# Score and transpose banks shared by a slot's two duos, and a new order of the last attention

## The reference

```python
x = x + attention(layernorm(x), ctx, ctx)      # below
x = x + ffn(layernorm(x))

# attention: q of 32 heads, k and v of 8 heads, each k and v head serves 4 q heads
q, k, v = (query @ Wq), (ctx @ Wk), (ctx @ Wv)
q, k = rope(q, positions), rope(k, positions)          # q * cos + rotate_half(q) * sin
scores = where(mask == 0, -1e9, q @ k.T / sqrt(128))
out = (softmax(scores) @ v) @ Wo                       # (.., 32 * 128) @ (4096, 512)

# ffn
routing = softmax(x @ gate_w.T)                        # 8 experts
out = (x * (routing @ in_scale)) @ sign(weight).T * (routing @ out_scale) + bias
```

## Time and profile before

| | us |
|---|---|
| median of 3 runs | 1307.17 (1306.85 to 1307.28) |
| the profiled execution | 1309.06 |
| its span, first to last instruction | 1307.2 |
| TensorE busy | 1192.8 (91%) |
| VectorE busy | 842.7 (64%) |
| GpSimd busy | 722.0 (55%) |
| ScalarE busy | 554.0 (42%) |
| mean granted clock of TensorE | 0.978 of full |

### The profile page before, as it was taken

How to read it: one execution, slowest core, us unless ns; L and a number is a source line. 1 busy time by engine, 2 the same in 40 slices (tenths; PEclk the granted TensorE clock), 3 DMA queues, 4 the chain that set the end, 5 groups by cost and what they waited for, 6 DMA issues and landing times.

```text
span 1307.2 us, 23826 instructions
## 1 busy us (share of the span) xinstructions
PE 1192.8 (91%) x7636; PEld 957.9 (73%) x7636; DVE 842.7 (64%) x1367; ACT 554.0 (42%) x1768; POOL 722.0 (55%) x593
## 2 busy tenths in 40 slices
PE   5799999999999999998999999999999999999977
PEld 4577777777777777776777777777777777777755
DVE  6667666666676666666666666656666666666644
ACT  3344444444434444443444444444444354344422
POOL 4566654554665554655455665545565655565424
PEclk8799999999999999999999999999999999999977
DMA  8233332222322222332322322323222222232100
GB/s 212 66 101 101 92 95 77 80 76 75 110 82 73 72 80 64 115 95 86 87 63 65 97 75 77 96 62 101 81 82 80 66 72 64 72 89 73 57 1 33
DMA packets 136924, 106.04 MB, mean 81 GB/s; under 512 B 12776, under 2 KB 111080, under 8 KB 136864
## 3 DMA queue, kind: packets, MB, share of 16 engines
q1 hardware_dynamic: 131488, 94.78, 25.0%
q10 hardware_dynamic: 4608, 8.39, 1.9%
q0 software_dynamic: 768, 2.10, 0.5%
HBM read 101.05 MB, written 4.19 MB: 81 GB/s over the span
## 4 chain that ended last, share of the span: by engine, by line
PE 66%; DVE 15%; ACT 7%; issue 7%; POOL 2%; ACTq 1%; DMA 1%; SPq 1%; DVEq 1%; POOLq 0%
PE chunk L1001 18%; PE chunk L1003 16%; PE chunk L1002 16%; ACT probs L529 5%; PE o_ps L1073 5%; PE sc_ps L1048 4%; PE tr_ps L990 3%; DVE scores L724 2%; DVE oT_lo L707 2%; DVE neg_max L729 1%; DVE acc L714 1%; DVE f_tile L813 1%; PE aux L1151 1%; DVE swp L773 1%; POOL y L430 1%
## 5 line engine op out<-in xcount | busy, mean ns | idle before, releaser
L396 POOL TENSOR_TENSOR w_lo<-raw,w_hi 128x512 fp32r<-128x512 f32 x192 | 256.6, 1343 | 473.1 <-ACT w_hi L495 472.6
L773 DVE TENSOR_TENSOR swp<-chunk,sinT 64x512 f32<-64x512 f32 x320 | 220.3, 689 | 42.6 <-PE chunk L1003 37.5
L529 ACT ACTIVATE probs<-scores,neg_max 128x64 f32<-128x64 f32 x512 | 171.0, 335 | 149.6 <-DVE neg_max L729 149.6
L1001 PE MATMUL chunk<-wo_hi,oT_hi 128*128 128x512 f32 x512 | 210.2, 411 | 1.8 <-issue 1.8
L1001 PE MATMUL chunk<-xT_hi,w_hi 128*128 128x512 f32 (+1 forms) x512 | 208.2, 407 | 0.2 <-DVE kT L775 0.2
L1003 PE MATMUL chunk<-wo_hi,oT_lo 128*128 128x512 f32 x512 | 201.6, 394 | 0.0
L1002 PE MATMUL chunk<-wo_lo,oT_hi 128*128 128x512 f32 x512 | 201.1, 393 | 0.0
L1002 PE MATMUL chunk<-xT_lo,w_hi 128*128 128x512 f32 (+1 forms) x512 | 200.9, 392 | 0.0
L1003 PE MATMUL chunk<-xT_hi,w_lo 128*128 128x512 f32 (+1 forms) x512 | 200.3, 391 | 0.0
L403 POOL TENSOR_TENSOR qT<-qT,swp 128x512 f32<-128x512 f32 x128 | 165.9, 1296 | 46.8 <-DVE qT L775 46.8
L396 POOL TENSOR_TENSOR wo_lo<-raw,wo_hi 128x512 fp32r<-128x512 f32 x132 | 170.2, 1290 | 20.6 <-ACT wo_hi L495 20.6
(11 more groups left out here) (266 smaller groups left out, 2005.2 us busy)
## 6 DMA issues: line engine op xcount, KB each, us to landing
raw<-in_L_xattn_Wo SPq DMA_DIRECT2D x132, 256.0 KB, 2.6
raw<-in_L_xattn_Wq SPq DMA_DIRECT2D x128, 256.0 KB, 2.7
raw<-in_L_xattn_Wk SPq DMA_DIRECT2D x32, 256.0 KB
raw<-in_L_xattn_Wv SPq DMA_DIRECT2D x32, 256.0 KB
acc<-in_x ACTq DMA_DIRECT2D x16, 256.0 KB, 2.8
c_tile<-in_ctx SPq DMA_DIRECT2D x12, 256.0 KB, 3.0
x_tile<-in_x SPq DMA_DIRECT2D x12, 256.0 KB, 3.5
result<-y ACTq DMA_DIRECT2D x12, 256.0 KB, 2.1
```

The source lines that it names most:

```text
L396: nc.gpsimd.tensor_tensor(lo, raw[:, n % RING, :], hi.bitcast(F32), ALU.subtract).then_inc(wsplit_lo, 1)
L529: last = nc.scalar.activation(probs[:, d, bass.ts(k, S)], scores[:, 2 * d + k // 4, bass.ts(k % 4, S)], ACT.Exp, bias=neg_max[:, d, k:k + ...
L773: last = nc.vector.tensor_tensor(swp[to, k, :], bank[of, :], sinT[to, here], ALU.mult)
L1001: nc.tensor.matmul(bank, a_hi, b_hi, start=i == 0, stop=False)
```

## The change

Both duos get banks of their own: scores and transposed probabilities of duo 0 use `sc_ps`, those of duo 1 `tr_ps`; the transposes of v use `o_ps[0]`, the rotary table rows `o_ps[1]`. The scores of both duos are issued one behind the other. The waits change with the banks: scores d wait for pT_lo d of the slot before, v_rows for the last out_lo of the slot before, values 0 for the rotary tables of an intake tile.

The orders in a slot change on four engines (TensorE's and GpSimd's are in the diff). ScalarE's is now: split_hi 0, 1, v_in_rows, split_hi 2, c_split, f_transposed, exp 0, exp 1, pT_hi 0, rope_tables, x_split, router_exp, split_hi 3, 4, pT_hi 1, out_hi 0, 1, route_hi, split_hi 5, 6, 7, xs_split, out_hi 2, 3, out_scales, split_hi 8, 9, v_out, store. Before, it was: v_in_rows, split_hi 0, 1, c_split, exp 0, split_hi 2, rope_tables, f_transposed, exp 1, x_split, pT_hi 0, router_exp, pT_hi 1, split_hi 3, 4, out_hi 0, 1, route_hi, split_hi 5, 6, out_hi 2, 3, split_hi 7, xs_split, out_scales, and the same end.

VectorE's is now: positions and stats, f_stats, f_norm, add_out 0, v_lo, soft_a 0, soft_a 1, c_lo, x_norm, add_out 1, soft_b 0, add_out 2, 3, soft_b 1, rotate 0, router_max, pT_lo 0, x_lo, routing, rotate 1, pT_lo 1, route_lo, out_lo 0, 1, rotate 2, scale_in, rotate 3, out_lo 2, 3, finish, rotate 4. Before: positions and stats, f_stats, add_out 0, v_lo, x_norm, c_lo, soft_a 0, f_norm, add_out 1, soft_b 0, add_out 2, soft_a 1, x_lo, add_out 3, pT_lo 0, router_max, soft_b 1, routing, rotate 0, pT_lo 1, out_lo 0, 1, rotate 1, route_lo, out_lo 2, 3, scale_in, rotate 2, rotate 3, finish, rotate 4.

Slot 32 gets an order of its own (`attend_last`) on three engines. The last wo is split into half of xT, which the last quarter doesn't use, and so waits for no reader; the xs buffers of the end move to the other half. Values 1 of the last attention go between the output products 0 and 1 of the final step, and add_bias moves from step 1 to step 4.

```diff
+        DUO_BANK, V_BANK, TABLE_BANK = [sc_ps, tr_ps], o_ps[0], o_ps[1]
...
-                             xT_hi[:, p, 0:E], xT_lo[:, p, 0:E],
+                             xT_hi[:, p, E:2 * E], xT_lo[:, p, E:2 * E],
...
+        last_wo_hi, last_wo_lo = xT_hi[:, :, 0:E], xT_lo[:, :, 0:E]
...
-                    hi, lo = wo_hi[:, c - PROJ, :], wo_lo[:, c - PROJ, :]
+                    hi, lo = (wo_hi, wo_lo) if s.proj else (last_wo_hi, last_wo_lo)
+                    hi, lo = hi[:, c - PROJ, :], lo[:, c - PROJ, :]
...
                     rope_sum(s, 0)
+                    rope_sum(s, 1)
                     split_lo(s, 5)
                     split_lo(s, 6)
-                    rope_sum(s, 1)
                     split_lo(s, 7)
                     rope_sum(s, 2)
                 if s.ffn:
                     xs_lo_split(f[0], in_slot)
                 if s.proj:
+                    rope_sum(s, 3)
                     split_lo(s, 8)
-                    rope_sum(s, 3)
                     split_lo(s, 9)
                     rope_sum(s, 4)
...
-                if step == 1:
+                if step == 4:
                     add_bias(f, place)
...
+                else:
+                    hi = last_wo_hi[:, c - PROJ, :]
...
+            def attend_last(s):
+                for n in range(HG):
+                    split_hi(s, n)
+                v_in_rows(s)
+                exp_duo(s, 0)
+                exp_duo(s, 1, range(4))
+                pT_hi_split(s, 0)
+                exp_duo(s, 1, range(4, 8))
+                out_hi(s, 0)
+                out_hi(s, 1)
+                pT_hi_split(s, 1)
...
-                if s.number == SLOTS:
-                    for n in range(HG):
-                        split_hi(s, n)
...
+                if step == 0 and p == 1:
+                    out_hi(last_attention, 2)
+                    out_hi(last_attention, 3)
...
+            def attend_last(s):
+                add_out(s, 0)
+                v_lo_split(s)
+                soft_a(s, 0)
+                soft_a(s, 1)
+                add_out(s, 1)
+                soft_b(s, 0)
+                add_out(s, 2)
+                pT_lo_split(s, 0)
+                add_out(s, 3)
+                soft_b(s, 1)
+                out_lo(s, 0)
+                out_lo(s, 1)
+                pT_lo_split(s, 1)
...
                     if p == 0:
+                        out_lo(last_attention, 2)
+                        out_lo(last_attention, 3)
                         dve.wait_ge(route_ok, 1)
                     f_norm(f, place, b)
...
             def v_rows(s):
 
                 pe.wait_ge(vT_ok, s.U)
                 if not s.first_attn:
-                    pe.wait_ge(pT_l, (s.U - 1) * DUOS)
+                    pe.wait_ge(o_lo, (s.U - 1) * PAIRS)
                 for p in range(PAIRS):
-                    last = transpose(tr_ps[:, bass.ts(p, D)], vT[:, bass.ts(p, P)])
+                    last = transpose(V_BANK[:, bass.ts(p, D)], vT[:, bass.ts(p, P)])
                 last.then_inc(v_tr, 1)
...
             def scores_of(s, d):
                 n = (s.U - 1) * DUOS + d
                 pe.wait_ge(roped, s.U * KQ)
-                if not (s.first_attn and d == 0):
-                    pe.wait_ge(masked, n)
+                if not s.first_attn:
+                    pe.wait_ge(pT_l, n - DUOS + 1)
...
-                                last = nc.tensor.matmul(sc_ps[a * S:(a + 1) * S, bass.ts(place, S)],
+                                last = nc.tensor.matmul(DUO_BANK[d][a * S:(a + 1) * S, bass.ts(place, S)],
...
             def probs_T(s, d):
                 n = (s.U - 1) * DUOS + d
                 pe.wait_ge(probs_ok, n + 1)
+                for k in range(4):
+                    last = transpose(DUO_BANK[d][:, bass.ts(k, P)], probs[:, d, bass.ts(k, P)])
+                last.then_inc(probs_tr, 1)
+
+            def values(s, d):
+
+                n = (s.U - 1) * DUOS + d
+                pe.wait_ge(pT_l, n + 1)
                 if d == 0:
                     pe.wait_ge(v_ok, s.U)
+                    if s.intake:
+                        pe.wait_ge(rope_ok, jobs_of(s)[0][0] + 1)
                 else:
-                    pe.wait_ge(pT_l, n)
-                for k in range(4):
-                    last = transpose(tr_ps[:, bass.ts(k, P)], probs[:, d, bass.ts(k, P)])
-                last.then_inc(probs_tr, 1)
-
-            def values(s, d):
-
-                n = (s.U - 1) * DUOS + d
-                pe.wait_ge(pT_l, n + 1)
-                if not (s.first_attn and d == 0):
                     pe.wait_ge(o_lo, 2 * n)
...
             def t_rows(t):
+                pe.wait_ge(rows_in, 16 * (t - PAIRS + 1))
+                transpose(TABLE_BANK[:, 0:P], rows[:, 0:P])
+                transpose(TABLE_BANK[:, P:2 * P], rows[:, P:2 * P]).then_inc(rows_tr, 1)
+
+            def t_x(t):
                 pe.wait_ge(c_lo, t + 1)
-                pe.wait_ge(rows_in, 16 * (t - PAIRS + 1))
-                transpose(aux[:, 0:P], rows[:, 0:P])
-                transpose(aux[:, P:2 * P], rows[:, P:2 * P]).then_inc(rows_tr, 1)
-
-            def t_x(t):
-                pe.wait_ge(rope_ok, t + 1)
                 pe.wait_ge(xn_ok, t + 1)
                 transpose_tile(aux, x_tile).then_inc(x_tr, 1)
...
+            def attend_last(s):
+                out_proj(s, 0)
+                v_rows(s)
+                scores_of(s, 0)
+                scores_of(s, 1)
+                out_proj(s, 1)
+                out_proj(s, 2)
+                probs_T(s, 0)
+                out_proj(s, 3)
+                values(s, 0)
+                probs_T(s, 1)
+
...
                 if s.attn:
                     v_rows(s)
                     scores_of(s, 0)
+                    scores_of(s, 1)
                 if s.intake:
                     t_context(t)
+                if s.ffn:
+                    t_f(f, in_slot)
                 if s.wo:
                     out_proj(s, 1)
+                    out_proj(s, 2)
+                    out_proj(s, 3)
+                if s.proj:
+                    project(s, 0)
+                if s.attn:
+                    probs_T(s, 0)
+                    probs_T(s, 1)
                 if s.intake:
                     t_rows(t)
-                if s.ffn:
-                    t_f(f, in_slot)
-                if s.wo:
-                    out_proj(s, 2)
-                if s.attn:
-                    scores_of(s, 1)
-                if s.intake:
                     t_x(t)
-                if s.wo:
-                    out_proj(s, 3)
-                if s.attn:
-                    probs_T(s, 0)
                 if s.ffn:
                     t_logits(f, in_slot)
                 if s.proj:
-                    project(s, 0)
-                if s.attn:
-                    probs_T(s, 1)
+                    project(s, 1)
+                if s.attn:
                     values(s, 0)
-                if s.proj:
-                    project(s, 1)
                 if s.ffn:
                     t_route(f, in_slot)
-                if s.attn:
-                    values(s, 1)
                 if s.proj:
                     project(s, 2)
                 if s.first_proj:
@@ -1205,6 +1249,8 @@
                     project(s, 3)
                 if s.ffn:
                     t_out_scales(f, in_slot)
+                if s.attn:
+                    values(s, 1)
                 if s.proj:
                     project(s, 4)
...
                 if step == 0:
+                    if p == 1:
+                        values(last_attention, 1)
                     out_proj(s, p)
```

More of the change, by code:

```diff
@@ L230, in run_slots @@
             quarter(eng, slot, QT - 1, True, False)
-            slot(Slot(QT, 0, False, False))
+            slot(last_attention)
             last_slot = Slot(QT, 1, False, False)
@@ L563, in rope_tables @@
                 act.wait_ge(rows_tr, t + 1)
-                scaled(cosT[:, span(place * P, P)], aux[:, 0:P])
-                scaled(sinT[:, span(place * P, P)], aux[:, P:2 * P]).then_inc(rope_ok, 1)
+                scaled(cosT[:, span(place * P, P)], TABLE_BANK[:, 0:P])
+                scaled(sinT[:, span(place * P, P)], TABLE_BANK[:, P:2 * P]).then_inc(rope_ok, 1)
             def x_split(t, place):
@@ L610, in slot @@
                     split_hi(s, 1)
-                if s.intake:
-                    c_split(*t)
                 if s.attn:
-                    exp_duo(s, 0)
+                    v_in_rows(s)
                 if s.proj:
@@ L617, in slot @@
                 if s.intake:
-                    rope_tables(*t)
+                    c_split(*t)
                 if s.ffn:
@@ L850, in slot @@
                     f_stats(*f, in_slot)
+                    f_norm(*f, in_slot)
                 if s.wo:
@@ L904, in slot @@
                     rotate(s, 3)
+                if s.attn:
+                    out_lo(s, 2)
+                    out_lo(s, 3)
                 if s.ffn:
```

99 lines of the change are left out of this document (49 added, 50 removed).

## The result

The kernel with the change takes 1199.83 us (median of four runs, 1198.69 to 1200.64), the kernel before beside it 1307.22. The ratio is 0.9178 with a 95% interval of 0.9162 to 0.9194. The profiled execution took 1200.44 us with a span of 1197.4.

A forecast was written before the change was run, and what follows sets the result against it. TensorE's queue, its own work and two or three waits a slot, was taken as the bound. Steady part 79, start 3 and end 11 make 93, less small waits 90 us: 1217 us, eight in ten 1206 to 1237.

The forecast's parts named there:

- What bounds the kernel: Steady part: set by TensorE's queue in its order, its own work and two or three waits a slot; 70.9 us idle.
- Walk through the slot: Steady part: waits at probs, values and f_tile go; split 9 about 0.3 us to spare; 0.35 charged at output scales.
- the sum of the steady part: Slots 2 to 32: intake slots 40 and sinT 2, plain slots 11, FFN slots 26; together 79 us, bounds 55 and 90.
- given back for small waits: Steady part: 0.1 us off the gain for each of 30 slots, for small waits that such a walk misses.
- Price of a visit: TensorE leaving its 512-column stream for small products: 0.2 us; one visit less in a plain slot, two in the others.
- Price of a wait: TensorE: a wait costs a little more than its bracket; 0.15 us added ahead of transposes.
- Start: Slots 0 and 1: projection 4's wait of some 2 us hides; slot 1 gains about 3 us, bounds 0 and 6.
- End: From slot 32's v_rows: final product 9.8 earlier, values 1 and out_lo -1.4, clock 1.8, norms 2, add_bias -1.2; 11 us.
- A: FFN slots keep a wait, 1.2 us more in each of 12: 1231 us; chance 0.2.
- B: A margin of 0.3 to 0.6 fails in every slot, at pT_lo 0 or split 9: 1243 us; chance 0.1.
- C: GpSimd's chain from rope_sum 1 to split 9 becomes the bound and the kernel slower, 1343 us; chance 0.03.
- D: More than worked out: end 14, no wait at the scales, no small waits, visits at full price: 1206 us; chance 0.12.

The follow-up runs named there:

- The first experiment: Scores 1 moved behind output product 1, in a visit of its own, in slots 1 to 31, against the changed kernel: 1210.33 us, 10.5 more.
- the second experiment: Both transposes of probabilities put ahead of projection 0 instead of behind it, against the changed kernel: 1249.08 us, 49 more.

## Why the prediction was right in kind and wrong in size

*What bounds the kernel* was right. The waits of the earlier trace rows set the time, and moving their readers behind work that was there anyway took all of them away. The order is the gain: the banks alone bring nothing, and each piece of the order that was taken back (the transposes, values 1, GpSimd's) brings a wait back.

*Walk through the slot.* Right at each point that was tested: no wait at probs, values 0, values 1 or f_tile; the output scales wait behind fT (0.33 late, 0.35 charged); split 9 keeps up. Split 9 ends 0.26 ahead of the output product in a plain slot (0.3 forecast), and this margin is thinner than it looks: GpSimd's old order, or values 1 moved by one projection, brings TensorE onto it. What the walk missed is the sign: the rope_sums moved forward don't use a margin up, they save a wait worth 0.42 that the shorter period would have brought in plain and intake slots.

*The step that failed: the sizes in the sum of the steady part, and slot 0 at nothing.* The steady part was put at 79 less 3 and gave 92.2, so 16.2 are missing. The start was put at 3 and gave 5.7, the end at 11 and gave 12.0. The mechanism held; no single price explains the difference, and every sizeable miss but one lies on the same side. To find the terms, each of TensorE's visits is timed in both traces, from the start of the last large matmul ahead of it to the start of the second one behind it, less two steps of 0.227; like visits with and without a wait then give what the wait cost, bracket or not.

| where the 16.2 lie | forecast | measured | more |
|---|---|---|---|
| waits on oT_lo ahead of values | 32.7 | 35.8 | 3.1 |
| waits ahead of x_tile and rows | 2 | 4.6 | 2.6 |
| waits ahead of probs and f_tile | 38.4 | 40.3 | 1.9 |
| visits | 10.8 | 13.1 | 2.3 |
| given back for small waits | -3 | 0 | 3.0 |
| slots 15 and 5, in no term | 0 | 3.5 | 3.5 |
| wait at the output scales | -4.2 | -5.3 | -1.1 |
| rounding of 79.7 to 79 | | | 0.7 |

These are 16.0 of the 16.2. The waits are the largest group. The prediction gave those ahead of values no more than their brackets, and they cost 0.07 more each, 0.13 in FFN slots; ahead of x_tile and rows it took 2 of 3.3 of brackets; ahead of transposes it added 0.15, where 0.2 is right. The 3 us given back for small waits that a walk misses did not come: but for the output scales and one gap at slot 15 TensorE waits for nothing in 30 slots.

*Price of a visit.* The first experiment gives 0.37 for 0.2, but this doesn't go to all 54 visits that the new order saves. In each slot one of scores went, and that saves about 0.35; the second one saved in intake and FFN slots is of transposes, and that is free by the second experiment. A plain slot saved 0.35 (0.2 forecast) and an intake slot 0.32 (0.4 forecast): two errors that nearly cancel. An FFN slot saved some 0.6 for 0.4, by an estimate, since two of its visits never came without a wait; 0.18 of it lies at the FFN product, which takes 2.05 before and 1.87 now with no bracket in either, and why is open.

*What the trace of before had by accident.* Slot 15 had 41.5 us against 37.8 for its like, with a gap that nothing released and a lower clock behind it; with the change the gap is at the same place, but short. From TensorE's timelines, before:

```profile
618.10 0.49 PE L1001 MATMUL chunk<-wo_hi,oT_hi 128*128 128x512 f32 x1 [1.81 <-issue]
...
618.89 0.57 PE L1001 MATMUL chunk<-wo_hi,oT_hi 128*128 128x512 f32 x1
```

and after:

```profile
565.56 0.49 PE L1037 MATMUL chunk<-wo_hi,oT_hi 128*128 128x512 f32 x1 [0.36 <-issue]
```

Slot 15 gave 3.1 us beyond an intake slot's gain and slot 5, whose clock was 0.96 before and 1.00 after, 0.4. The gap belongs to the old order, the clock does not: with the banks alone the gap is 1.82 at the same place, the granted clock stays at 1.00, and slot 15 has 39.9 us. So about half of the 3.1 is the gap and half the clock, which in that run fell in six other slots instead. In none of the traces of the new order does it fall in these 30 slots. Why the issue gap shrank is open: it is 0.20 to 0.44 in five other runs of the new order, so it goes with the order. What in it does that was not tried.

*Price of a wait.* Close ahead of values (the bracket and 0.07; the prediction took the bracket), a little low ahead of transposes (0.2 for 0.15), and too low ahead of a product: three experiments give the bracket and 0.25.

*Start.* Slot 1 gave 2.7 (3 forecast). Slot 0 gave 3.0 where nothing was forecast, of which GpSimd's old order alone gives back 2.2. The prediction saw that projection 4 would wait some 2 us (it waits 1.87) and that this would hide behind rotate 3 at projection 5. It left out the clock. The long gap ahead of projection 5 went, so that product ran at the upper clock and the slow stretch fell on projection 4, which had time. The first two lines are TensorE's timeline in the changed kernel, in projections 4 and 5:

```profile
42.42 0.63 PE L1039 MATMUL chunk<-xT_hi,w_lo 128*128 128x512 f32 x1
42.86 0.61 PE L1037 MATMUL chunk<-cT_hi,w_hi 128*128 128x512 f32 x1
43.31 0.40 PE L1038 MATMUL chunk<-cT_lo,w_hi 128*128 128x512 f32 x1
```

Before, projection 5 went at 0.63 a matmul, one each 0.43, from 43.47 on, and v_rows followed at 49.74. Now it starts 0.6 us earlier and takes 12 times 0.2 less; these are the 3.0. In the run with add_bias back at step 1, whose slot 0 is the same, the clock doesn't fall on projection 4 at all, and v_rows of slot 1 start at 46.83, where the changed kernel has 46.75: it is projection 5 that counts. The two stretches by window, 44 to 50 us (PE, PEld, DVE, ACT, POOL, clock), before and after:

```profile
44.00:50.00 6.00, 5.22 (x15) 3.63 (x14) 1.52 (x3) 0.60 (x1) 3.32 (x3) 0.59 0.29 87
```

```profile
44.00:50.00 6.00, 4.55 (x77) 3.68 (x75) 2.48 (x4) 2.64 (x5) 6.00 (x6) 1.00 0.29 90
```

*End.* 12.0 against 11. The final product came 10.0 earlier (9.8 forecast). Of the other four terms (-1.4, 1.8, 2, -1.2, together 1.2) the sum came out at 2.0, but not term by term: the move of add_bias, credited with 0.8, is worth 0. Three norms were expected to become short, and the one that stays at 1.48 is that on which the last tile's path hangs.
The Trainium skill, "SBUF — State Buffer", "Who interferes with whom", has the rule that was used for this. The traces agree: the last norm takes 1.48 with GpSimd's add beside it and 0.55 without.

*Rivals.* A: FFN slots keep a wait of 0.18, not 1.2. B and C: no w_lo or wo_lo waited for in the steady part. D, more than worked out (1206, chance 0.12), is what happened, by more than it allowed: of its terms no small waits came true, but the wait at the scales stayed and the end gave 12, not 14, and it had neither the undercounted waits nor the start's clock nor slot 15.

Of the 109.8 us of span, 2.4 don't show in the medians: the time around the span grew from 1.9 to 3.0, and the profiled execution of before lies 1.8 above its median, that of after 0.6.

## What to carry to other kernels

Where one engine is busy at 91% and each of its waits has a named releaser, walk one period with durations from the trace, and move each reader behind work that is there anyway; a new bank is worth only the order that it permits. Price a visit of small matmuls in a stream of large ones from a run, since no bracket shows it, and by its kind, since one of scores had a price here and one of transposes had none. Count every wait, the small ones too, and take its price from like instructions with and without it, not from the bracket. And at each gap look at the clock behind it: which work then runs at the low level can be worth more than the gap.

## What the runs showed of the hardware that was not expected

- Leaving a stream of 512-column matmuls for 32 of 64 columns and coming back costs 0.37 us, none of it shown as idle. Leaving it for transposes of 128 columns costs nothing: apart or together with others they take the same time within 0.01 (0.57 from rows to the next product in both).
- A wait ahead of a 512-column product costs its bracket and about 0.25 us (0.15 cost 0.42, 0.18 cost 0.44, 0.85 cost 1.10); ahead of values it costs the bracket and 0.05 to 0.07 (0.63 cost 0.68, 1.14 cost 1.21).
- TensorE starts about 0.14 us after the GpSimd instruction that it waits for has ended (0.10 to 0.15 in two runs), so a margin of 0.26 in the trace had 0.12 to spare.
- A gap of TensorE with no releaser lies at one output product behind slot 15's projections. It takes 1.8 us in the old order and 0.2 to 0.44 in six of the runs of the new. A fall of the clock came behind it in the kernel before (matmuls at 0.57), and none with the banks alone, where the gap is as long.
